# Attention and mixture of experts on one core: norm weights folded, output halves summed on the way out of PSUM, projection over 256 rows

## The chip, the cores and the metric

One core of a Trainium2 chip runs the whole program. The metric is the device time of one execution in microseconds (us). The engines are called PE (matmul and transpose; PEld is its weight load), DVE (VectorE), ACT (ScalarE), POOL (GpSimd) and SP (SyncE, which here only issues DMAs).

## What is computed

The input is x of 8 batches x 256 tokens x 256 features. Two layers follow. The first one is an attention of 16 heads with rotary parts (`L0_attn`) gated by a quantised feed-forward (`L0_ffn`); the change touches it only in a constant and in how the weights of the second layer are prepared. The second layer, cut to what matters:

```python
qkv = einsum('bld,ed->ble', x, w_qkv)         # x here: layer-normalised rows
q = rmsnorm(q, q_norm_w); k = rmsnorm(k, k_norm_w)   # over D = 16, H = 16 heads
scores = einsum('bhqd,bhkd->bhqk', q, k) * D ** -0.5
attn = softmax(scores)
out = einsum('bhqk,bhkd->bhqd', attn, v).transpose(0, 2, 1, 3).reshape(B, L, dim)
attn_out = einsum('bld,ed->ble', out, w_proj) + b_proj
# beside it: 8 routed experts of width 176 (top 2) and a shared one of 352
```

The result of the mixture goes through a gate, is multiplied with attn_out and added to x.

## The kernel before

Every value that enters a matmul is split into a high and a low part of a reduced type (fp32r): ACT copies the high part, DVE or POOL subtracts to get the low one. `product` (lines 55 to 60) makes three matmuls from one: high x high, high x low, low x high. So an operand that comes out of PSUM costs an ACT and a DVE or POOL operation before it can be used.

Three stages run one after the other, each a block with one program per engine. `stage_first` is the feed-forward of layer 0; beside it, ACT and POOL split the weights of the later stages piece by piece (`PIECES`) and SP stores them (`w1_scratch`, `wp_scratch`, ...). POOL also makes nqk = q_norm_w * k_norm_w * scale there, a tile of 128 x 256. `stage_attention0` is the attention of layer 0. `stage_layer1` (line 1079 on) does the second layer.

`stage_layer1` runs over slots n from -16 to 132. Slot n = 16 b + u carries the scores of head u of batch b for n from 0 to 127, and on each engine it does a fixed list in a fixed order. A head's way: scores on PE (L1836, ahead by a slot), negative maximum on DVE (L1696), exponentials on ACT (L1487), reciprocal on DVE (L1728), normalisation on POOL (L1376), transposes on PE (`turn`, L1846), high part on ACT (L1495) and low part on DVE (L1700), product with the values on PE (`values`, L1860). There is one PSUM bank each for scores, turn and output (PO).

Between these each slot has items, taken from `attn_jobs` and from the list of pieces of the mixture. Items of the attention are Q0, Q1, V (projections of the next batch), T (transposes of the normalised rows), X0, X1 (transposes of the scaled q and k), P0, P1 (output projection), L and C (router logits, combine weights). Pieces of the mixture are g, G, u, U (gate and up of a tile, halves of the contraction) and D0, D1 (down). The planner gives each item a cost in units (`COST`) and adds pieces to a slot while the credit of `SLOT_GOAL` units holds, of which 10 (`UNIT`) are the head's own work. The items' PSUM banks are three, in the order of the list (`JOB`, `job_free`).

q and k of a batch: DVE sums the squares (`sum_squares`, L1622), POOL makes three Newton steps (`root_rms`), DVE scales the rows (`scale_rows`, L1635), POOL multiplies q with nqk (`weigh`, L1356), PE transposes (X, L1788, waits for "weighted" and "k_scaled"), ACT and DVE split (L1459, L1575), SP stores to memory (`store_stack`, eight DMAs) and loads the operands of the scores from there, two pairs of heads at a time (`load_stack`, five DMAs). SP's program is one list in which a load that is not due holds back all behind it; `stack_until` puts the stack's transfers between the weight loads, by slot.

The output: four heads share PO. v is spread by POOL over zeroed columns (`vp`) so that head e of a group of four writes 32 rows of PO: 16 for the high part of v and 16 for the low. ACT copies PO to `ot` high (`out_hi`, L1501), DVE subtracts to `ot` low (`out_lo`, L1671). The projection sums high and low rows of four groups, 4 x 128 rows, with the rows of w_proj given twice (`proj_rows`).

## Time and profile before

| what | us |
|---|---|
| median of 3 runs | 1403.62 (1402.06 to 1404.83) |
| the profiled execution | 1404.14 |
| its span | 1402.3 |
| PE busy | 1349.8 (96%) |
| DVE, ACT, POOL busy | 910.4, 752.8, 738.1 |
| second layer: first scores | at 931.97 |

Times in rows are microseconds from the start of the span. "Idle before" is the time an engine did nothing ahead of an instruction, with what ended it. Matmuls overlap, so their durations add up to more than the time between their starts.

### The profile page before, as it was taken

Reading aid. Unit: us, or ns where it says so; the run is one execution under the profiler, and the core shown is the slowest. Engines: PE = TensorE matmul, PEld = TensorE weight load, DVE = VectorE, ACT = ScalarE, POOL = GpSimd, SP = SyncE. Lnnn points to the kernel's source line nnn. Section 1 sums busy time; section 2 is a strip of 40 time slices with the busy share of each in tenths; the row PEclk is TensorE's granted clock in tenths of the full one; section 3 lists DMA queues with packets and bytes.
Section 4 is the critical chain, followed back from the end, with each engine's and each line's share of the span. In section 5 each row is a group of like instructions: output and inputs, shape, how many; then the busy total and the mean of one; then the engine's idle time right before and its main releaser. Section 6 shows DMA issues by size and latency. Waiting matters only on the chain. (4 is left out here: it accounts for less than half of the span.)

```text
span 1402.3 us, 25300 instructions
## 1 busy us (share of the span) xinstructions
PE 1349.8 (96%) x8758; PEld 1201.7 (86%) x8758; DVE 910.4 (65%) x1793; ACT 752.8 (54%) x1948; POOL 738.1 (53%) x725
## 2 busy tenths in 40 slices
PE   9999899999999999999999999879999999999898
PEld 7887798999899989998999898668888888889797
DVE  6655566556656665666565665557887777786765
ACT  4553444545544555445544544246666666666664
POOL 1651333554444545434645453448658676866775
PEclk9999999999999999999999999999999999999999
DMA  5995333324332343233324424166555653645572
GB/s 191 328 329 201 83 91 93 89 77 121 106 89 49 102 138 92 62 90 104 106 65 119 119 65 170 67 173 188 145 177 162 188 173 105 205 149 168 174 196 90
DMA packets 105645, 190.78 MB, mean 136 GB/s; under 512 B 20304, under 2 KB 39440, under 8 KB 103216
## 3 DMA queue, kind: packets, MB, share of 16 engines
q1 hardware_dynamic: 105520, 189.17, 45.0%
q8 instruction: 71, 1.16, 0.4%
q14 instruction: 54, 0.44, 0.1%
HBM read 116.68 MB, written 30.47 MB: 105 GB/s over the span
## 5 line engine op out<-in xcount | busy, mean ns | idle before, releaser
L775 POOL TENSOR_TENSOR a_pr<-a_pr,a_ri 128x512 f32<-128x512 f32 x128 | 133.2, 1041 | 299.5 <-DVE a_ri L955 299.5
L832 ACT ACTIVATE a_pr<-a_score,a_nb 128x256 f32<-128x256 f32 x256 | 119.0, 470 | 267.6 <-DVE a_nb L947 267.6
L1376 POOL TENSOR_TENSOR l_pr<-l_pr,l_ri 128x512 f32<-128x512 f32 x128 | 133.2, 1040 | 121.5 <-DVE l_ri L1728 119.5
L1487 ACT ACTIVATE l_pr<-l_score,l_nb 128x256 f32<-128x256 f32 x256 | 119.1, 471 | 107.7 <-DVE l_nb L1696 107.6
L58 PE MATMUL a_job<-s_xs,s_wh 128*128 128x512 f32 x384 | 153.8, 401 | 1.0 <-PEq L221 1.0
L60 PE MATMUL a_job<-s_xs,s_wl 128*128 128x512 f32 x384 | 151.7, 395 | 0.0
L59 PE MATMUL a_job<-s_xs,s_wh 128*128 128x512 f32 x384 | 151.3, 394 | 0.0
L947 DVE TENSOR_REDUCE a_nb<-a_score 128x2 f32<-128x512 f32 x128 | 88.5, 691 | 85.8 <-PE a_score L1026 84.1
L1696 DVE TENSOR_REDUCE l_nb<-l_score 128x2 f32<-128x512 f32 x128 | 87.5, 684 | 39.4 <-PE l_score L1836 39.2
L960 DVE TENSOR_TENSOR a_pt<-a_turn,a_pt 128x512 fp32r<-128x512 f32 x128 | 87.5, 684 | 23.7 <-ACT a_pt L840 23.7
L1495 ACT ACTIVATE s_wh<-l_turn 128x512 fp32r<-128x512 f32 x128 | 76.9, 600 | 36.3 <-PE l_turn L1846 36.3
L1700 DVE TENSOR_TENSOR s_wh<-l_turn,s_wh 128x512 fp32r<-128x512 f32 x128 | 87.3, 682 | 8.2 <-ACT s_wh L1495 7.7
L1860 PE MATMUL l_out<-s_wh,l_vp 128*128 128x256 f32 x512 | 91.7, 300 | 0.2 <-DVE s_wh L1700 0.2
L58 PE MATMUL l_job<-l_xs,s_wl 128*128 128x512 f32 x224 | 89.6, 400 | 1.9 <-DVE l_vc L1570 1.9
L1846 PE MATMUL l_turn<-s_ident,l_pr 128*128 128x128 f32 x512 | 78.1, 275 | 11.5 <-DVE s_wh L1700 11.1
L60 PE MATMUL l_job<-l_xs,s_wl 128*128 128x512 f32 x224 | 89.0, 397 | 0.0
L59 PE MATMUL l_job<-l_xs,s_wl 128*128 128x512 f32 x224 | 88.6, 396 | 0.0
L955 DVE RECIPROCAL a_ri<-a_sm 128x2 f32<-128x2 f32 x128 | 21.3, 166 | 102.1 <-ACT a_pr L832 102.1
L60 PEld LDWEIGHTS a_job<-s_xs,s_wl 128*128 128x128 f32 x384 | 72.1, 188 | 16.9
L1846 PEld LDWEIGHTS l_turn<-s_ident,l_pr 128*128 128x128 f32 x512 | 58.7, 140 | 29.5 <-issue 14.0
L58 PEld LDWEIGHTS a_job<-s_xs,s_wh 128*128 128x128 f32 x384 | 72.2, 188 | 11.3 <-issue 1.4
L59 PEld LDWEIGHTS a_job<-s_xs,s_wh 128*128 128x128 f32 x384 | 72.4, 189 | 10.3
(251 smaller groups left out, 4569.2 us busy)
## 6 DMA issues: line engine op xcount, KB each, us to landing
s_wl<-wgu_scratch SPq DMA_DIRECT2D x56, 512.0 KB, 5.7
a_sk<-a_rotk SPq DMA_DIRECT2D x384, 64.0 KB, 2.0
a_sq<-a_rotq SPq DMA_DIRECT2D x256, 64.0 KB, 2.0
s_xs<-xn_scratch SPq DMA_DIRECT2D x14, 1024.0 KB, 5.7
l_wd<-wd_scratch SPq DMA_DIRECT2D x56, 256.0 KB, 2.9
l_zq<-qs_scratch SPq DMA_DIRECT2D x128, 64.0 KB, 4.3
l_sk<-ks_scratch SPq DMA_DIRECT2D x32, 256.0 KB, 4.9
a_raw<-in_w SPq DMA_DIRECT2D x30, 256.0 KB, 3.0
```

The lines of the kernel that those rows point to most:

```text
L58: pe.matmul(out, lh, rh, start=first, stop=False)
L59: pe.matmul(out, lh, rl, start=False, stop=False)
L60: return pe.matmul(out, ll, rh, start=False, stop=last)
L775: pool.tensor_tensor(e, e, ri[:, n % 2, :].unsqueeze(2).broadcast_to([P, 2, SEQ]), ALU.mult)\
L832: i = act.activation(pr[:, n % 2, t, :], PS[n % 2][:, t * SEQ:(t + 1) * SEQ], ACT.Exp, bias=nb[:, n % 2, t:t + 1], accum_out=sm[:, n % 2, ...
L947: dve.tensor_reduce(nb[:, (n + 1) % 2, :], PS[(n + 1) % 2][:, :].rearrange("p (t k) -> p t k", t=2), AX.X, ALU.max, negate=True).then_inc( ...
L960: dve.tensor_tensor(pt[:, n % 2, 1, :], PT[:, :], pt[:, n % 2, 0, :], ALU.subtract).then_inc(S["turn_free"], 1)
L1376: pool.tensor_tensor(e, e, ri[:, n % 3, :].unsqueeze(2).broadcast_to([P, 2, SEQ]), ALU.mult)\
L1487: i = act.activation(pr[:, n % 3, t, :], PS[n % NPS][:, t * SEQ:(t + 1) * SEQ], ACT.Exp, bias=nb[:, n % 3, t:t + 1], accum_out=sm[:, n % 3 ...
L1696: dve.tensor_reduce(nb[:, (n + 1) % 3, :], PS[(n + 1) % NPS][:, :].rearrange("p (t k) -> p t k", t=2), AX.X, ALU.max, negate=True).then_in ...
L1846: i = pe.transpose(PT[:, kc * SEQ + t * P:kc * SEQ + (t + 1) * P], pr[:, n % 3, t, kc * P:(kc + 1) * P], ident[:, :])
L1860: i = pe.matmul(PO[:, 0:SEQ], vp[:, kc, a, e * P:(e + 1) * P], pt[:, n % 2, q, kc * SEQ:(kc + 1) * SEQ], start=(e == 0 and kc == 0 and q = ...
```

## The change

It folds nqk into the transposed q: the tile becomes one value for each of 128 rows, and X's copy and subtraction carry it as a scale, so each becomes two operations (q with, k without). `weigh` goes. The first batch has both squares in slot -12, both scalings in slot -9, its X one slot earlier, its first stack loads in slot -5 and not -4, and the two memsets of `zq` on POOL. The columns of `vp` are laid out so that the high parts of a group's four heads fill 64 rows of PO and the low parts the other 64. ACT copies one half, DVE adds the other and writes 64 rows of `os`; two groups make 128 rows, which ACT copies (high) and POOL subtracts (low) once in eight slots. P0 and P1 then contract over two blocks of 128 rows and not four, and come in slots u = 4, 5 and not 3, 4 (but for the last batch). Their cost is 6 units for 12, and the goal of a slot 28.1 for 28.7.

```diff
-VG, VSTRIDE, VBLK = 4, 160, 640
+VG, VB, VSTRIDE, VBLK = 4, 2, 144, 576
+VHALF = VG * D1
-        self.wp = sh.wl[:, 0:2 * VG * D].rearrange("p (q a d) -> p q a d", q=2, a=VG)
+        self.wp = sh.wl[:, 0:2 * VB * D].rearrange("p (q a d) -> p q a d", q=2, a=VB)
-        + [("w", i) for i in range(KC)] + [("p", i) for i in range(2)]
+        + [("w", i) for i in range(KC)] + [("p", 0)]
...
-                        pool.tensor_tensor(sh.nqk[:, :], nw[:, 0:D], nw[:, D:2 * D], ALU.mult).then_inc(S["nqk_raw"], 1)
+                        pool.tensor_tensor(sh.nqk[:, :], nw[:, 0:1], nw[:, 1:2], ALU.mult).then_inc(S["nqk_raw"], 1)
...
-                for i in range(2):
-                    sp.dma_start(l1.wp[:, :, 2 * i:2 * i + 2].bitcast(F32).rearrange("p s a d -> p s (a d)"), wp_dram[i]).then_inc(l1.w_in, 16)
+                sp.dma_start(l1.wp.bitcast(F32).rearrange("p s a d -> p s (a d)"), wp_dram[0]).then_inc(l1.w_in, 16)
...
-    T, Q, V, S_, P_, LOG, CMB, GU, DH = 4, 12, 12, 4, 12, 20, 4, 12, 6
+    T, Q, V, S_, P_, LOG, CMB, GU, DH = 4, 12, 12, 4, 6, 20, 4, 12, 6
-    UNIT, SLOT_GOAL, EARLY_GOAL = 10, 28.7, 18
+    UNIT, SLOT_GOAL, EARLY_GOAL = 10, 28.1, 18
     def X_AT(m):
-        return (9, 10)
+        return (8, 9) if m == 0 else (9, 10)
-        if u in (3, 4) and b >= 1:
-            jobs.append((f"P{u - 3}", b - 1))
+        first = 3 if b == BATCH else 4
+        if u in (first, first + 1) and b >= 1:
+            jobs.append((f"P{u - first}", b - 1))
+        ITEMS[n].sort(key=lambda item: item in (("X0", 0), ("X1", 0)))
+    LOAD_AT = {2 * PER_LOAD * i - (4 if i else 5): i for i in range(N // (2 * PER_LOAD))}
...
-                    if n % (2 * PER_LOAD) == 0 and 0 <= n // (2 * PER_LOAD) + 1 < N // (2 * PER_LOAD):
-                        load_stack(n // (2 * PER_LOAD) + 1)
+                    if n in LOAD_AT:
+                        load_stack(LOAD_AT[n])
...
-                def weigh(m):
-                    pool.wait_ge(S["q_scaled"], m + 1)
-                    pool.tensor_tensor(qk[:, 0], qk[:, 0], sh.nqk[:, :].unsqueeze(1).broadcast_to([P, TB, D]), ALU.mult)\
-                        .then_inc(S["weighted"], 1)
+                def out_lo(k):
+                    pool.wait_ge(S["out_hi"], k + 1)
+                    pool.tensor_tensor(ot[:, 1, k % VB, :], os[:, k % VB, :], ot[:, 0, k % VB, :], ALU.subtract).then_inc(S["out_lo"], 1)
...
                 pool.memset(vp[:, :, :, :].bitcast(F32), 0.0).then_inc(S["vp_zeroed"], 1)
+                pool.wait_ge(S["vp_zeroed"], 1)
+                pool.memset(zq[64:P, 0].bitcast(F32), 0.0).then_inc(S["zeroed"], 1)
+                pool.wait_ge(S["zeroed"], 1)
+                pool.memset(zq[0:64, 1].bitcast(F32), 0.0).then_inc(S["zeroed"], 1)
...
                     if 0 <= n + 1 < N:
                         normalise(n + 1)
+                    if n >= 10 and (n - 10) % 8 == 0 and (n - 10) // 8 < VB * BATCH:
+                        out_lo((n - 10) // 8)
                     for K in HID_AT[n]:
                         hid_lo(K)
...
-                        act.activation(tqk[:, half, :, 0, :], bank[:, :].rearrange("p (r n) -> p r n", r=2), ACT.Copy).then_inc(S["turned_hi"], 1)
+                        act.activation(tqk[:, half, 0, 0, :], bank[:, 0:SEQ], ACT.Copy, scale=sh.nqk[:, 0:1])
+                        act.activation(tqk[:, half, 1, 0, :], bank[:, SEQ:2 * SEQ], ACT.Copy).then_inc(S["turned_hi"], 1)
...
-                def out_hi(g):
+                def out_low(g):
+                    here, there = VHALF * (g % 2), VHALF * (1 - g % 2)
                     act.wait_ge(S["pv_done"], 4 * g + 4)
-                    if g >= VG:
-                        wait_full(act, ("P1", g // VG - 1))
-                    act.activation(ot[:, 0, g % VG, :], PO[:, 0:SEQ], ACT.Copy).then_inc(S["out_hi"], 1)
+                    act.activation(ol[here:here + VHALF, :], PO[there:there + VHALF, 0:SEQ], ACT.Copy).then_inc(S["out_low"], 1)
+
+                def out_hi(k):
+                    act.wait_ge(S["out_free"], 2 * k + 2)
+                    if k >= VB:
+                        wait_full(act, ("P1", k // VB - 1))
+                    act.activation(ot[:, 0, k % VB, :], os[:, k % VB, :], ACT.Copy).then_inc(S["out_hi"], 1)
...
                     if n >= 6 and (n - 6) % 4 == 0 and (n - 6) // 4 < VG * BATCH:
-                        out_hi((n - 6) // 4)
+                        out_low((n - 6) // 4)
                     if 0 <= n + 1 < N:
                         exps(n + 1)
+                    if n >= 10 and (n - 10) % 8 == 0 and (n - 10) // 8 < VB * BATCH:
+                        out_hi((n - 10) // 8)
...
-                def out_lo(g):
-                    dve.wait_ge(S["out_hi"], g + 1)
-                    dve.tensor_tensor(ot[:, 1, g % VG, :], PO[:, 0:SEQ], ot[:, 0, g % VG, :], ALU.subtract).then_inc(S["out_free"], 1)
+                def out_sum(g):
+                    here = VHALF * (g % 2)
+                    dve.wait_ge(S["out_low"], g + 1)
+                    if g >= 4:
+                        dve.wait_ge(S["out_lo"], (g - 4) // 2 + 1)
+                    dve.tensor_tensor(os[here:here + VHALF, g // 2 % VB, :], PO[here:here + VHALF, 0:SEQ], ol[here:here + VHALF, :], ALU.add)\
+                       .then_inc(S["out_free"], 1)
...
-                        if u in ((4, 5) if b < 0 else (2, 3)):
-                            sum_squares(b + 1, u - (4 if b < 0 else 2))
-                        if u == 4 and b < 0:
-                            dve.memset(zq[64:P, 0].bitcast(F32), 0.0).then_inc(S["zeroed"], 1)
-                            dve.memset(zq[0:64, 1].bitcast(F32), 0.0).then_inc(S["zeroed"], 1)
-                        if u in (7, 8):
-                            scale_rows(b + 1, u - 7)
+                        for r in range(2):
+                            if u == (4 if b < 0 else 2 + r):
+                                sum_squares(b + 1, r)
+                        for r in range(2):
+                            if u == (7 if b < 0 else 7 + r):
+                                scale_rows(b + 1, r)
...
-                        pe.wait_ge(S["out_free"], VG * (m + 1))
-                        for a in range(VG):
+                        pe.wait_ge(S["out_lo"], VB * (m + 1))
+                        for a in range(VB):
                             i = product(pe, bank[:, 0:D], [ot[:, q, a, t * P:(t + 1) * P] for q in range(2)],
-                                        [wp[:, q, a, :] for q in range(2)], a == 0, a == VG - 1)
+                                        [wp[:, q, a, :] for q in range(2)], a == 0, a == VB - 1)
```

DVE's subtraction of X is split in the same way as ACT's copy (a `scalar_tensor_tensor` with nqk for q, a `tensor_tensor` for k), and the rows of w_proj in `proj_rows` are given once, eight heads to a block.

## Rows read from the trace of the kernel before

**Rows 1.** The page's head.
```profile
span 1402.3 us, 25300 instructions
```

**Rows 2.** Stretches of the span: PE, PEld, DVE, ACT, POOL busy; clock; DMA share; GB/s.
```profile
932.00:1380.40 448.40, 429.14 (x2927) 383.59 (x2928) 337.42 (x738) 294.56 (x839) 317.45 (x387) 0.99 0.57 169
1380.40:1402.30 21.90, 15.82 (x112) 14.31 (x110) 10.29 (x18) 6.36 (x15) 9.47 (x8) 0.97 0.15 48
```

**Rows 3.** Timeline of the last projection: start, duration, engine, line; 20 starts lie between.
```profile
1394.79 0.28 PE L58 MATMUL l_job<-s_wl,l_ot 128*128 128x256 f32 x1
...
1397.16 0.28 PE L60 MATMUL l_job<-s_wl,l_ot 128*128 128x256 f32 x1
```

**Rows 4.** The chain that ended last, around the first scores: start, time, work.
```profile
901.04 0.91 DVE l_zq L1718
902.67 1.10 DVE l_ss L1622
...
909.59 0.75 DVE l_qk L1635
...
912.46 1.68 DVE l_qk L1635
914.27 0.63 PE l_job L1788 x4
926.38 5.46 DMA l_sk<-ks_scratch
931.97 0.77 PE l_score L1836 x2
```

**Rows 5.** PE ahead of and behind the first scores: timeline, then stretches with granted clock.
```profile
906.50 0.50 PE L58 MATMUL l_job<-l_xs,s_wl 128*128 128x512 f32 x1 [1.92 <-DVE l_vc L1570]
...
936.38 0.52 PE L1836 MATMUL l_score<-l_sk,l_zq 128*128 128x256 f32 x2
...
912.00:914.00 2.00, 0.00 (x0) 1.00 0.11 45
...
930.00:931.00 1.00, 0.00 (x0) 0.50 1.03 336
```

**Rows 6.** SP's issues and POOL's first product with a combine row, in the first batch.
```profile
916.29 0.56 SPq L1271 DMA_DIRECT2D qs_scratch<-l_tqk  x1
...
921.98 0.53 SPq L1256 DMA_DIRECT2D ct_scratch<-l_ct  x1
923.64 0.36 SPq L1265 DMA_DIRECT2D l_cb<-ct_scratch  x1
...
924.52 1.82 SPq L1286 DMA_DIRECT2D l_zq<-qs_scratch  x4
...
927.81 1.26 POOL L1383 TENSOR_TENSOR l_ga<-l_ga,l_cb 128x512 f32<-128x512 f32 x1 [6.70 <-DMA l_cb<-ct_scratch]
```

**Rows 7.** PE's waits in the body (total, times, longest); POOL's product; DVE's scaling, min/median/max.
```profile
PE l_turn L1846 <- DVE s_wh L1700: 11.1, 25, 1.3
...
PE l_job L1788 <- issue: 3.2, 5, 0.7
...
L1356 POOL TENSOR_TENSOR l_qk<-l_qk,s_nqk 128x512 f32<-128x512 f32 x8 | 13.1, 1633 | 0.0
...
L1635 DVE TENSOR_TENSOR l_qk<-l_qk,l_rq x16: 679/812/1827, 909.6 to 1307.9; 128x512 f32<-128x512 f32 x16
```

**Rows 8.** Groups of instructions: count, busy us, mean ns of one, idle before.
```profile
L1387 POOL TENSOR_TENSOR l_hid<-l_ga,l_hid 128x512 fp32r<-128x512 f32 x56 | 72.0, 1285 | 6.3 <-ACT l_hid L1510 6.2
L1501 ACT ACTIVATE l_ot<-l_out 128x256 fp32r<-128x256 f32 x32 | 12.6, 394 | 1.6 <-PE l_out L1860 1.6
L1459 ACT ACTIVATE l_tqk<-l_job 128x512 fp32r<-128x512 f32 x16 | 9.5, 593 | 2.5 <-PE l_job L1788 2.5
```

**Rows 9.** Timeline of the end: POOL's last merge and DVE's last product.
```profile
1396.59 1.29 POOL L1399 TENSOR_TENSOR s_x<-s_x,l_y 128x512 f32<-128x512 f32 x1
...
1398.36 0.69 DVE L1737 TENSOR_TENSOR l_y<-l_y,l_s 128x512 f32<-128x512 f32 x1
```

More of the change, by code:

```diff
@@ L98, in __init__ @@
         self.ident = n.sb("ident", [P, P])
-        self.nqk, self.bp, self.db = (n.sb(s, [P, D]) for s in ("nqk", "bp", "db"))
+        self.bp, self.db = (n.sb(s, [P, D]) for s in ("bp", "db"))
+        self.nqk = n.sb("nqk", [P, 1])
         self.rw = n.sb("rw", [P, 2, KC, E], F32R)
@@ L163, in stage_first @@
     NHID, NRAW, NSPLIT = 3, 4, 3
-    PIECES = [("g", i) for i in range(2)] + [("m", i) for i in range(MT)] + [("w", i) for i in range(KC)] + [("p", i) for i in range(2)]
+    PIECES = [("g", i) for i in range(2)] + [("m", i) for i in range(MT)] + [("w", i) for i in range(KC)] + [("p", 0)]
     PIECES = [("g", 0), ("g", 1)] + [x for i in range(8) for x in (("m", i), ("g", i + 2))] + [("m", i) for i in range(8, MT)] \
-        + [("w", i) for i in range(KC)] + [("p", i) for i in range(2)]
+        + [("w", i) for i in range(KC)] + [("p", 0)]
     PIECE_AT = {}
@@ L1205, in stage_layer1 @@
             "own", "consts", "zeroed", "vp_zeroed", "job_full", "xs_hi", "v_hi", "spread",
-            "sq_ready", "ms_ready", "newton", "q_scaled", "k_scaled", "weighted", "turned_hi",
+            "sq_ready", "ms_ready", "newton", "q_scaled", "k_scaled", "turned_hi",
             "score_full", "max_ready", "exp_ready", "sum_inv", "norm_ready", "turn_full", "turn_hi", "turn_free",
-            "pv_done", "out_hi", "out_free", "tanh_ready", "gate_done", "cmul", "hid_hi", "hid_lo", "down_done",
+            "pv_done", "out_low", "out_free", "out_hi", "out_lo", "tanh_ready", "gate_done", "cmul", "hid_hi", "hid_lo", "down_done",
             "lg_exp", "cm_ready", "y_ready", "y_tanh", "y_act", "gated", "merged", "last_merged", "stored")}
@@ L1574, in job_out @@
                         dve.wait_ge(S["turned_hi"], 2 * m + half + 1)
-                        dve.tensor_tensor(tqk[:, half, :, 1, :], bank[:, :].rearrange("p (r n) -> p r n", r=2),
-                                          tqk[:, half, :, 0, :], ALU.subtract).then_inc(free_of(item), 1)
+                        dve.scalar_tensor_tensor(out=tqk[:, half, 0, 1, :], in0=bank[:, 0:SEQ], scalar=sh.nqk[:, 0:1],
+                                                 in1=tqk[:, half, 0, 0, :], op0=ALU.mult, op1=ALU.subtract)
+                        dve.tensor_tensor(tqk[:, half, 1, 1, :], bank[:, SEQ:2 * SEQ], tqk[:, half, 1, 0, :], ALU.subtract).then_inc(free_of(item), 1)
                     elif name[0] == "P":
@@ L1705, in _ @@
                     if n >= 6 and (n - 6) % 4 == 0 and (n - 6) // 4 < VG * BATCH:
-                        out_lo((n - 6) // 4)
+                        out_sum((n - 6) // 4)
                     if n - 1 in SUM_AT and SUM_AT[n - 1] == NSTEP - 1:
@@ L1782, in do_item @@
                         half = int(name[1])
-                        pe.wait_ge(S["weighted"], m + 1)
+                        pe.wait_ge(S["q_scaled"], m + 1)
                         pe.wait_ge(S["k_scaled"], m + 1)
@@ L1926, in proj_rows @@
     import numpy as np
-    rows = [[(VG * a + p // (2 * D1)) * D1 + p % D1 for p in range(P)] for a in range(VG)]
+    rows = [[(2 * VG * j + p // D1) * D1 + p % D1 for p in range(P)] for j in range(VB)]
     return np.concatenate([w[r] for r in rows], axis=1)
@@ L1986 @@
         "w_qkv": head_columns(i["L1_attn_w_qkv"]).T, "w_proj": proj_rows(i["L1_attn_w_proj"].T),
-        "norm_w": _np.concatenate([_np.tile(_np.repeat(i[f"L1_attn_{s}_norm_w"], 4), 4) for s in "qk"])[None],
+        "norm_w": _np.stack([_np.tile(_np.repeat(i[f"L1_attn_{s}_norm_w"], 4), 2) for s in "qk"], axis=1),
         "b_proj": i["L1_attn_b_proj"][None],
```

14 lines of the change are left out of this document (7 added, 7 removed).

## The prediction

> **What bounds the kernel now.** I read the page's head first, then the stretches of the second layer, then the timelines of the places where PE stands still. The profiled execution took 1404.14 us, of which 1402.3 are the span [rows 1]; the median of the runs is 1403.62, so the sum is made against 1404.14 and 0.5 us come off at the end. In the 448.4 us from the first scores to the last ones PE is busy for 429.14, DVE for 337.42, POOL for 317.45 and ACT for 294.56 [rows 2]. So PE bounds the body: a matmul taken away there is time, nearly one for one, and work added to another engine is free until it holds back something that PE is due to take. Ahead of the body is a stretch that PE does not bound: a chain of DVE, POOL, PE, SP and DMA that ends in the first scores at 931.97, some 5 us after PE's last piece [rows 4, 5]. Behind it are the last 21.9 us, with PE busy for 15.8 [rows 2].
>
> **The projection.** Each of 16 items P0/P1 is 12 matmuls of 256 columns and becomes 6. Between the first row of [rows 3] and the last lie 20 such starts in 2.37 us, 0.118 each, so an item falls from 1.42 to 0.71 us. 14 items lie in the body: 9.9 us. The planner's goal of 28.7 to 28.1 units a slot spreads the freed room: a unit is about one such matmul, and 0.6 x 0.118 x 128 slots is 9.1, the same thing from the other side; the last D1 then comes in slot 128, not 129. It is not one for one, since each slot gets shorter while DVE's work in it does not, and PE is busy for 96%. I take nine tenths, **-8.9**; ends -5 and -10.5.
>
> **The weights folded.** POOL's product of q with nqk goes: 8 times 1633 ns [rows 7]. In the body it stands right ahead of X0, and the five waits of PE put down to "issue" there, 3.2 us together [rows 7], are for it by the code (X waits for "weighted"). Beside it DVE's scaling of rows took up to 1827 ns, where its shortest is 679 [rows 7], and what is queued behind it reaches the next slot's turn late. I count the 3.2 and 1.3 for those, **-4.5**; ends -1 (X0 waits for the scaled k instead) and -8. In its place X's copy on ACT becomes two, 2 x 394 for 593 ns [rows 8], so 16 x 0.2 = 3.1 us on an engine that is busy for 66% of the body; DVE's subtraction becomes two as well, by the same proportion 0.2 more each. X's bank is then free 0.4 us later, with three banks in turn, and its stores that much later, with the loads due three slots on: **+0.5**, ends 0 and +3.
>
> **The output.** ACT's first copy keeps its time (half the partitions, 256 elements, 394 ns [rows 8]), and so does DVE's operation on PSUM. New are 16 copies on ACT from SBUF (394 ns, the nearest row) and 16 subtractions on POOL, at half of 1285 ns [rows 8] 0.65 each, 10.3 us, under the 13.1 that leave. ACT's second copy waits for DVE's sum; behind it on ACT are a gate's tanh and a hidden tile's copy. On POOL the subtraction stands behind the slot's normalisation and ahead of the hidden tile's low half. P waits for out_lo of slot u = 2 and comes in u = 4, so a slot of 448.4/127 = 3.5 us covers a chain of some 2 us. I take **+1**; from below 0, from above 16 x 0.65 = 10. What decides is DVE's 1827 against 679 ns beside a POOL operation [rows 7]: POOL work of 10.3 us replaces 13.1 of the same kind. The Trainium skill, SBUF — State Buffer, section "Who interferes with whom", says that a DVE instruction with two SBUF inputs and a GpSimd instruction that reads SBUF exclude each other for a whole instruction. By that page the subtraction, moved from DVE on PSUM to POOL on SBUF, speaks against this change, and up to 10 us would come back.
>
> **The first batch.** Now: squares of row 0, two memsets of 0.91 us on DVE, squares of row 1 at 902.67, Newton steps on POOL, scaling at 909.59 and 912.46, product, X0 at 914.27 [rows 4]. After the change the second squares follow the first directly and end at 900.6, not 903.8; Newton and the small steps around it take the 5.8 us up to 909.59 and so end at 906.4. V's output, no longer behind the second squares, comes 2 us sooner, and g1, which waited until 906.50 for it [rows 5], with it. DVE is through U0 near 907.1 and scales both rows by 908.9, so X0 is issued near 909, 5.3 us sooner. Routing, G1 and U1 stand ahead of X0's subtractions on DVE: out at 912.9 (before: by 916.29 [rows 6]); X1, whose bank waits for U1, at 914.4. The memsets go to POOL: no row prices them there; between 0.9 us (DVE's) and 2.6 (POOL's 1285 ns for half the columns [rows 8]) each. I take 0.9, done before Newton wants POOL; at 2.6 Newton starts 3 us late.
> On SP four stores of each half take 0.6 us each to issue [rows 6], so the last ends near 917.8. Now the combine's store goes at 921.98, its load at 923.64, the stack's loads at 924.52 [rows 6]; with these due a slot sooner they stand ahead of that store and start near 918.3. sk, issued at 926.38, led to scores 5.6 us later [rows 4]; so the first scores could start near 925.75, 6.2 us sooner. PE's items up to there end near 924.7 (16.5 us of matmuls from 904.4 and some 3.8 of waits), so its idle 5 us shrink to 1. The granted clock was 0.50 (1.2 of 2.4 GHz) at 930 to 931, and the slot from 931.97 to 936.38 took 4.4 us where its matmuls need 2.4 at full rate; in the 3 us without a matmul ahead of X0 the clock stayed at 1.00 [rows 4, 5]. A short idle keeps PE at 2.4 GHz: 2.0 more, 8.2 in all.
> **What is late next** is the first routed expert: D0 of tile 3, in the slot of the first scores, needs POOL's product with the combine row, which started at 927.81, 4.2 us after its load was issued [rows 6]. That load now comes behind five loads, near 922.4: landed at 926.5, product 1.3, ACT 0.6, low half 1.3, so D0 at 929.8, where PE would be there at 927.4. PE loses 2.4 us of the 8.2, and slot 0 starts at 930.5 instead of 936.38 [rows 5]: **-5.9**, ends -3 and -8.5.
>
> **The rest.** At the end, D1 of the last tile now stands ahead of the last turn (+0.7), and the last output goes through ACT, DVE, ACT, POOL (0.4, 0.4, 0.4, 0.65 and hops, 2.0 us), so P0 starts 0.9 us later than now, and the two items are 1.4 us shorter: -0.5. But POOL's last merge, now at 1396.59, comes 0.7 later too, beside DVE's last product at 1398.36 [rows 9]: **0**, ends -0.5 and +1. The first stage splits one piece fewer and reads a far smaller norm_w, on ACT, POOL and SP while PE multiplies: 0, ends -0.5 and +0.5. If PE's wait for it were the last there, the whole gain of a smaller load would be in those 0.5. Sum: -8.9 - 4.5 + 0.5 + 1 - 5.9 = **-17.8**, so 1386.3 on the profiled execution and **1386** against the median.
>
> **The rivals.**
> (A) The body follows DVE, not PE. For it: the turn's 25 waits for DVE's low half, 11.1 us, are the body's largest idle [rows 7]. Against: 96%. Then the projection gives -5 and the product -2: 1404.1 - 5 - 2 + 1.5 - 5.9 = 1392.7, 1392 by the median.
> (B) More than forecast: the X slots lose all their waits (-8) and the combine's load lands in time (-8.2): 1404.1 - 9.9 - 8 - 8.2 + 1 = 1379.
> (C) Slower, by ACT's queue: out_hi waits there for DVE's sum with hid_hi, tanh and the next turn's copy behind it, and POOL's subtraction delays hid_lo, so that D waits. It makes the kernel slower when one of 16 such places costs over (17.8 + 1)/16 = 1.2 us; at twice its own work (2 x (0.39 + 0.65) = 2.1 us) the time is 1404.1 - 18.8 + 33 = 1418. Against it: ACT is idle for a third of the body, and a D follows its U by a slot or more.
> (D) It does not do what it says: the loads of the first stack land no sooner and the freed units turn into idle; -2 to -4, so 1401.
>
> **How the numbers follow.** Forecast (1381 to 1391) 0.54; A (to 1396) 0.20; B 0.17; D 0.05, half of it within 0.2% (2.8 us, about what a measurement of this kernel can tell from no change); C 0.04. The range 1378 to 1394 takes in B's 1379, A's 1392 and the first batch's bounds. Faster 0.94, same 0.03, slower 0.03.
>
> **What would show it.** First scores near 926, the clock at 1.00 through 940; PE waiting about 2 us for POOL's low half at the first routed D; no idle "issue" ahead of X0; 96 matmuls fewer on the three product lines; 435 us from first to last scores for 448.4. It is wrong if the first scores come after 929, if PE's idle in the body grows by over 5 us, or if turns wait on DVE in the slots of out_hi.

## The result, and the profile after

Four runs of the changed kernel gave a median of **1411.09 us** (1407.11 to 1412.16), beside 1403.11 for the kernel before in runs on the same chip: ratio **1.0045** [1.0032, 1.0058]. The change makes the kernel 0.45% slower, 8 us, where 17.8 us less were forecast. The profiled execution took 1407.11, the fastest of the four, so the trace shows some 3 of the 8 us. The mean granted clock of the four was 0.994, 0.991, 0.990 and 0.989, from the fastest to the slowest; the kernel before had 0.997 in its profiled execution, and 0.995 by the median of its executions in the batches below.

The page's head, to stand beside [rows 1] and the table of before:

```profile
span 1405.0 us, 25173 instructions
PE 1345.8 (96%) x8662; PEld 1194.3 (85%) x8662; DVE 911.1 (65%) x1807; ACT 765.2 (54%) x1979; POOL 736.7 (52%) x734
```

The work went as the diff says: PE's busy time fell by 4 us and its share is 96% as before. The stretches of the second layer in the changed kernel (busy time of PE, PEld, DVE, ACT, POOL, clock, DMA share, GB/s), from layer 1's first transposes to the first scores, on to slot 0, the body, the end, to stand beside [rows 2]:

```profile
889.13:921.97 32.84, 30.49 (x167) 24.48 (x167) 21.14 (x56) 12.51 (x24) 15.31 (x23) 1.00 0.38 129
921.97:931.17 9.20, 4.46 (x14) 3.69 (x15) 1.34 (x3) 2.58 (x7) 4.63 (x6) 0.65 0.88 268
931.17:1381.57 450.40, 420.91 (x2833) 373.22 (x2833) 339.37 (x751) 304.20 (x863) 315.17 (x392) 0.99 0.55 166
1381.57:1405.00 23.43, 14.17 (x97) 12.28 (x95) 11.45 (x18) 6.76 (x16) 10.12 (x9) 0.95 0.13 44
```

First scores came at 921.97, not 931.97; slot 0 at 931.17, not 936.38 [rows 5]. Then the body of 126 slots took 450.40 us, where before it took 444.0 (936.38 to 1380.39), with less PE work in it. The sum of PE's waits in this body, to stand beside [rows 7]:

```profile
PE l_turn L1867 <- DVE s_wh L1722: 18.6, 30, 2.1
PE l_down L1777 <- DVE l_y L1700: 4.9, 2, 3.6
PE l_job L1822 <- DVE l_xs L1583: 3.3, 3, 1.3
```

The waits for "issue" ahead of X are gone, as forecast. The turn's waits for DVE grew from 11.1 to 18.6, and two waits that were worth nothing before now cost 8.2 together.

**Where in the body.** From PE's timeline I took the start of the first score matmul of each slot, and so each slot's length. Slots with the same u have the same work for the attention; summed over slots 0 to 125 (us):

| kernel | u 3-5 | 6-8 | 9-10 | 11-12 | 13-15 | 0-2 | body |
|---|---|---|---|---|---|---|---|
| before | 83.9 | 83.0 | 63.2 | 57.3 | 74.9 | 81.7 | 444.0 |
| the change | 89.2 | 87.1 | 55.4 | 58.8 | 80.1 | 79.9 | 450.4 |

So the halved projection (u 3 to 5) made its own slots longer; the folded weights show their gain at u 9-10; and u 6-8 and 13-15, where the diff changes little but the planner's choices, grew by 9. The largest single place is slot 29, 8.56 us for 3.25. PE's timeline there:

```profile
1037.46 0.55 PE L1777 MATMUL l_down<-l_wd,l_hid 128*128 128x256 f32 x1 [3.57 <-DVE l_y L1700]
1037.81 0.41 PE L1778 MATMUL l_down<-l_wd,l_hid 128*128 128x256 f32 x1
...
1042.28 0.28 PE L1777 MATMUL l_down<-l_wd,l_hid 128*128 128x256 f32 x1
```

D0 of a group's first tile may start only when DVE has taken the last group's sum out of its bank (L1700). The new cost and goal moved D0 to the head of slot 29; before, it came later. PE stood 3.57 us, and the next matmuls took 0.41 for 0.28 us; the granted clock in these stretches of the changed kernel:

```profile
1036.00:1037.00 1.00, 0.00 (x0) 0.00 (x0) 1.00 (x3) 0.84 (x4) 0.00 (x0) 1.00 0.00 0
...
1038.00:1039.00 1.00, 1.00 (x7) 1.00 (x6) 0.00 (x0) 0.58 (x1) 0.94 (x1) 0.50 0.06 16
```

**The clock in the body, which this one trace shows at its mildest.** Behind its first 0.4 us, this body had a granted clock of 0.50 twice: at 1037.4 to 1040.8, and at 1081.7 to 1085.1, behind a turn's wait of 2.09 us for DVE. PE was busy for 6.7 us of it. In the kernel before the clock was at half only in the body's first 0.24 us. The variant with the loads in slot -4 (below) has the same items in its body, and its profiled execution took 1412.02. There such stretches add up to 17 us:

```profile
1036.85:1043.68 6.83, 5.90 (x22) 5.25 (x23) 2.20 (x5) 2.47 (x7) 1.04 (x1) 0.50 0.01 2
1125.60:1129.01 3.41, 3.41 (x18) 3.41 (x18) 1.49 (x6) 0.72 (x2) 3.10 (x7) 0.50 0.02 4
1241.65:1248.48 6.83, 6.83 (x34) 6.83 (x34) 3.71 (x15) 2.64 (x11) 4.76 (x11) 0.50 0.00 0
```

Slot 84, first in the change's trace, then in that variant's. The longest wait in it is the same, 1.28 and 1.27 us for T's low part (`l_xs`, L1583):

```profile
1235.87:1241.01 5.14, 3.86 (x35) 3.69 (x34) 4.65 (x13) 2.77 (x8) 3.46 (x5) 1.00 0.36 84
1238.28:1244.93 6.65, 5.38 (x34) 5.20 (x33) 4.71 (x13) 3.10 (x9) 4.74 (x8) 0.75 0.33 91
```

It took 5.14 us at a clock of 1.00, and 6.65 at 0.75; slot 85 behind it took 3.28 and 4.87. So the same work with the same waits was 3.1 us dearer in one execution than in the other, and one trace does not give the price of the change. Matmuls of 256 columns start 0.21 us apart at half clock, for 0.12 at full; so, as an estimate, the 16.1 us in which PE was busy in the three stretches cost some 7, where the 6.7 of the change's own trace cost some 3.

**Where the first batch's gain stopped.** SP's issues and PE's first item behind the first scores, in the changed kernel:

```profile
915.21 0.60 SPq L1277 DMA_DIRECT2D ks_scratch<-l_tqk  x1
...
916.48 1.84 SPq L1291 DMA_DIRECT2D l_zq<-qs_scratch  x4
918.37 0.56 SPq L1293 DMA_DIRECT2D l_sk<-ks_scratch  x1
...
921.34 0.35 SPq L1270 DMA_DIRECT2D l_cb<-ct_scratch  x1
921.74 0.42 SPq L1250 DMA_DIRECT2D s_wl<-wgu_scratch  x1
...
927.19 0.77 PE L59 MATMUL l_job<-l_xs,s_wl 128*128 128x512 f32 x1 [4.75 <-DMA s_wl<-wgu_scratch]
```

The stores ended at 915.8, 2 us before my estimate, and the scores came 3.8 us before it. But the gate and up weights of tile 5 are issued behind the stack's loads, the combine row's store and its load, at 921.74, and PE stood 4.75 us for them.

### The profile page after: what moved, and what is told of

Read it like the earlier page. It is cut to its first block and busy times, and to the rows that moved or that the text cites. A ratio compares the mean times of both kernels' runs of the same rounds, so it can differ in the third digit from the quotient of the medians.

```text
span 1405.0 us, 25173 instructions
## 1 busy us (share of the span) xinstructions
PE 1345.8 (96%) x8662; PEld 1194.3 (85%) x8662; DVE 911.1 (65%) x1807; ACT 765.2 (54%) x1979; POOL 736.7 (52%) x734
## 5 line engine op out<-in xcount | busy, mean ns | idle before, releaser
L1867 PE MATMUL l_turn<-s_ident,l_pr 128*128 128x128 f32 x512 | 78.1, 275 | 19.4 <-DVE s_wh L1722 18.6
L60 PEld LDWEIGHTS a_job<-s_xs,s_wh 128*128 128x128 f32 x384 | 72.2, 188 | 10.5
```

What stands on the lines that cost most here:

```text
L60: pe.matmul(out, lh, rl, start=False, stop=False)
L1867: i = pe.transpose(PT[:, kc * SEQ + t * P:kc * SEQ + (t + 1) * P], pr[:, n % 3, t, kc * P:(kc + 1) * P], ident[:, :])
```

## The experiments

Unless it is said otherwise, medians stand beside the kernel before in the same batch, ratios with their 95% interval. Bodies and slots are from the profiled execution of each.

### The planner's two numbers

**The change without them** (P costs 12 again, goal 28.7):

```diff
-    T, Q, V, S_, P_, ... = 4, 12, 12, 4, 6, ...
-    UNIT, SLOT_GOAL, EARLY_GOAL = 10, 28.1, 18
+    T, Q, V, S_, P_, ... = 4, 12, 12, 4, 12, ...
+    UNIT, SLOT_GOAL, EARLY_GOAL = 10, 28.7, 18
```

> The change with only the planner's two numbers put back (P cost 12 and SLOT_GOAL 28.7 units); P keeps its slots 4 and 5 and its 6 matmuls. Theory PLAN (the new numbers line pieces of the mixture up behind ACT, DVE and POOL work, above all D0 of tile 14 first in slot 29, where it waited 3.57 us for the sum of y): the body loses most of its extra stalls, first to last scores 450.4 us falls to 432 to 440, time 1393 to 1400. Theory OUTPUT (the longer chain ACT, DVE, ACT, POOL and the extra operations make the stalls): stalls stay, time 1407 or more.

1410.0, ratio 1.0039 [1.0024, 1.0054]. The old numbers alone give back about 1 us (the change had 1.0045). Slot 29 is back at 3.28 us, and the body is still 453.9: now u 11-12 take 63.2 for 58.8. Of the body's 3.5 us above the change's, some 3 are the clock: PE was busy at 0.50 for 13.0 us, for 7.1 there.

**The kernel before with only the two new numbers** (the reverse edit):

> The kernel before with only the planner's two numbers of the change (P cost 6, SLOT_GOAL 28.1), its P items still 12 matmuls in slots 3 and 4. Theory PLAN: slower than before, by 8 to 20 us (1411 to 1423), with stalls of PE on DVE's low half of the turn grown by 5 us or more. Theory OUTPUT: within 3 us of before, 1400 to 1406.

1413.04 for 1404.66, ratio 1.0058 [1.0043, 1.0073]: two constants, nothing else, cost 8 us. Slot 29 took 8.62 us here too.

**The change with D0 of a group's first tile last in its slot**, where the planner puts it first (slots 29 and 66):

```diff
+    for s in range(1, NSTEP):
+        for n in SLOTS:
+            if ("D0", MT * s) in ITEMS[n] and ITEMS[n][0] == ("D0", MT * s):
+                ITEMS[n] = ITEMS[n][1:] + ITEMS[n][:1]
```

> The change with D0 of the first tile of a step put last in its slot where it stood first (slots 29 and 66), so that DVE's sum of y is done when PE asks. Theory PLAN for slot 29 (excess 5.4 us, PE idle 3.57 and then at half clock): 4 to 6 us faster than the change, 1404 to 1407. If the sum of y holds back what follows anyhow: the same as the change.

1406.62 for 1404.39, ratio 1.002 [1.0009, 1.0031]: against the change's 1.0045 some 3.5 us better. The wait is shorter, not gone:

```profile
1038.65 0.36 PE L1781 MATMUL l_down<-l_wd,l_hid 128*128 128x256 f32 x1 [2.19 <-DVE l_y L1704]
```

Slot 29 took 6.22 us for 8.56. The body is as long as the change's all the same, 450.7: slots 21, 53 and 85 took 4.80, 4.38 and 4.80 us for 3.27 in the change's trace, with the granted clock at 0.50 for a part of each.

### The projection alone

Half of P's matmuls taken out of the kernel before, every copy and subtraction left in place (the sum runs over two of the four groups, so half of the projection is left out):

```diff
-                        for a in range(VG):
+                        for a in range(2):
```

> The kernel before with each P item multiplying two of its four blocks (the output leaves out half of the attention's projection), nothing else changed: 6 matmuls for 12 in slots 3 and 4, the output's chain as before. If PE bounds those slots: 9 to 10 us less, 1394. If DVE bounds them (90% busy in the slots 35 and 36 of the kernel before): the time falls by 0 to 3 us, 1401 to 1404, and the slots u = 3 and 4 keep their lengths, with PE idle.

1402.18 for 1404.61, ratio 0.9982 [0.9971, 0.9994]: **2.4 us**, where 8.9 were forecast of 9.9. The two slots 35 and 36 hold P0 and P1 of a batch. First the stretch in the kernel before, and, for comparison, one without T or P:

```profile
1059.26:1066.10 6.84, 6.62 (x54) 6.01 (x52) 6.15 (x16) 4.24 (x13) 4.82 (x5) 1.00 0.84 230
...
1141.00:1160.80 19.80, 19.80 (x137) 18.19 (x136) 14.32 (x32) 14.60 (x42) 12.35 (x14) 1.00 0.68 214
```

and the same two slots with half of P:

```profile
1059.42:1066.30 6.88, 5.44 (x42) 4.66 (x41) 6.18 (x16) 4.26 (x13) 4.82 (x5) 1.00 0.82 226
```

Twelve matmuls fewer, PE busy for 1.2 us less, and the slots not a moment shorter: DVE is busy for 6.15 us of 6.84, 90%, where in the stretch without T or P it is busy for 72%. Its timeline in slots 51 and 52 of the kernel before shows with what:

```profile
1117.19 0.69 DVE L1696 TENSOR_REDUCE l_nb<-l_score 128x2 f32<-128x512 f32 x1
1117.80 0.68 DVE L1700 TENSOR_TENSOR s_wh<-l_turn,s_wh 128x512 fp32r<-128x512 f32 x1
1118.39 1.13 DVE L1622 TENSOR_REDUCE l_ss<-l_sqr 128x32 f32<-128x512 f32 x1
...
1119.87 0.68 DVE L1566 TENSOR_TENSOR l_xs<-l_job,l_xs 128x512 fp32r<-128x512 f32 x1
...
1120.54 0.40 DVE L1583 SCALAR_TENSOR_TENSOR l_s<-l_job,s_bp 128x256 f32<-128x256 f32 x1
```

The squares of a row of q and k (1.1 us, one row in each of the slots u = 2 and 3), T's low part and the projection's own output come in these slots. They are DVE's. The projection's matmuls filled PE's time beneath them and were nearly free: PE's turns wait longer for DVE instead, 16.8 us in this body for 11.1.

**With the planner's new numbers** on top (half of the projection left out again):

> As e13 with the planner's two numbers of the change (P cost 6, goal 28.1), so that the freed room is filled with the mixture's pieces. If filling gives the room back: 8 us or more less than e13. If the new plan costs what it did in e2 (+8 with 12 matmuls): about the same as e13 or slower, 1402 to 1410.

1407.08, ratio 1.0017 [1.0004, 1.0029]: 4.9 us above the kernel with half of P alone. So the numbers cost 5 even where the matmuls that they count are gone.

### The weights folded, and the first batch

**The fold alone, on the kernel before** (nqk as one value for each row, `weigh` gone, X split in two on ACT and DVE):

```diff
-                        act.activation(tqk[:, half, :, 0, :], bank..., ACT.Copy)
+                        act.activation(tqk[:, half, 0, 0, :], bank[:, 0:SEQ], ACT.Copy, scale=sh.nqk[:, 0:1])
+                        act.activation(tqk[:, half, 1, 0, :], bank[:, SEQ:2 * SEQ], ACT.Copy)
...
-                            weigh(b + 1)
```

> The kernel before with the norm weights folded and nothing else (same plan). My term: -4.5 + 0.5, so 1399, ends 1395 and 1405; the five waits issue ahead of X0 (3.2 us) gone. If the split of X on ACT and DVE is what costs: 1403 to 1407.

**1398.95** for 1404.66, ratio 0.9959 [0.9943, 0.9975]: -5.7, forecast -4.0. PE's waits in this body (935.6 to 1376.4), where the "issue" line is gone and the turn's wait is as before:

```profile
PE l_turn L1842 <- DVE s_wh L1696: 10.9, 28, 1.2
PE l_down L1752 <- DVE l_y L1674: 1.4, 2, 0.7
PE l_score L1832 <- DMA l_sk<-ks_scratch: 0.6, 1, 0.6
PE l_job L1784 <- DVE l_qk L1631: 0.6, 1, 0.6
```

Slots u 9-10 fell from 63.2 to 57.9, and u 11-12 grew by 1.8. I put these down to the split of X, counted at 0.5; no run has the fold without the split.

**The change with the first batch as before** (both squares, scaling, X and the loads back in their slots; the two memsets stay on POOL):

> The change with its first batch put back (squares, scaling, X and stack loads in the slots of before; the memsets stay on POOL). Theory FIRST GAINS (slot 0 started at 931.2 in the change and at 936.4 before): 4 to 6 us slower than the change, 1414 to 1416. Rival (the clock's fall and the wait of 4.75 us for the gate weights of tile 5 behind the stack's loads take the gain back): the same as the change within 2 us.

1411.8, ratio 1.0046 [1.0029, 1.0063]: level with the change's 1.0045. Slot 0 starts at 931.87, only 0.7 us later than in the change, although its first scores come at 928.11 and not at 921.97: here the slot of the first scores takes 3.77 us, in the change 9.20.

**The change with the first stack's loads in slot -4 again**:

> The change with the first stack's loads due in slot -4 again and not -5 (all else as the change). Its slot of the first scores took 9.2 us, 4.75 of it waiting for the gate weights of tile 5, whose load stood behind five stack loads. If that order is the cause: weights and combine rows land sooner, first scores 1 to 3 us later, slot 0 starts at 929 to 931 and the time is the same or 1 to 2 us less. Rival (DMA queues are full whatever the order): the wait moves to the stack's own landing, slot 0 at 932 to 934, the time 1 to 2 us more.

1409.92 for 1403.55, ratio 1.0039 [1.0026, 1.0051]; first scores at 927.41 for 921.97, slot 0 at 931.48 for 931.17. Loads a slot sooner bring the first scores 5.4 us sooner and slot 0 only 0.3.

**Fold and first batch together, on the kernel before**:

> The kernel before with the fold and the change's first batch, without the output's half. The change's slot 0 started 3.6 us sooner after its stage's begin than before, e3's 1.3 us sooner. Theory FIRST GAINS: 1 to 3 us less than e3 (1396 to 1398 where e3 had 1399). Rival (given back in the slot of the first scores, as e4 suggested): e3 within 1 us.

1398.64 for 1404.61, ratio 0.9956 [0.994, 0.9973], beside 0.9959 for the fold alone. The first scores come at 925.02 for 931.29 with the fold alone, slot 0 at 934.61 for 935.69, 1.1 us sooner; the last scores come 0.4 sooner (1375.87, 1376.31), and the medians differ by 0.3.

### The output's two parts

**The output half alone, on the kernel before**: groups of two blocks, ACT, DVE, ACT, POOL, P0 and P1 of six matmuls in u = 3, 4, the planner's old numbers.

```diff
+                    act.activation(ol[here:here + VHALF, :], PO[there:there + VHALF, 0:SEQ], ACT.Copy)
+                    dve.tensor_tensor(os[here:here + VHALF, g // 2 % VB, :], PO[...], ol[...], ALU.add)
+                    act.activation(ot[:, 0, k % VB, :], os[:, k % VB, :], ACT.Copy)
+                    pool.tensor_tensor(ot[:, 1, k % VB, :], os[...], ot[:, 0, k % VB, :], ALU.subtract)
```

> The kernel before with only the output's half of the change (vp's layout, sum leaving PSUM, P over 256 rows), every item in the slot of before (P in 3 and 4, cost 12, goal 28.7) and the weights' product kept on POOL; zq's memsets on POOL. 14 items in the body are 0.71 us shorter. Theory OUTPUT (the longer chain stalls the slots u = 10 to 12, where ACT copies os ahead of X1 and DVE's reciprocal waits behind X1's subtraction): the slots 10 to 12 of each batch lose 1 us or more beyond before, time 1400 to 1406. Theory PLAN alone: 1393 to 1396.

1413.74 for 1403.55, ratio 1.0069 [1.0054, 1.0084].

**The same with the fold**:

> As the kernel before in plan and first batch, with both the fold and the output's half of the change (so all the change's arithmetic and none of its placement). If the parts add up (fold gave -5.7 alone): e5 less 5.7. Theory PLAN: 1388 to 1391. Theory OUTPUT with X's split (both load ACT in slot 10): 1398 to 1404, and less than the sum of the parts' gains.

1409.0, ratio 1.0039 [1.0027, 1.005]. The fold gives its 5 us again; against the fold alone the output half **costs 11** (ratios 1.0039 and 0.9959), although it takes away the matmuls that were worth 2.4. PE and POOL in slot 35 of this kernel:

```profile
1059.94 0.36 PE L59 MATMUL l_job<-s_wl,l_ot 128*128 128x256 f32 x1 [2.38 <-POOL l_ot L1380]
```

```profile
1058.07 1.04 POOL L1375 TENSOR_TENSOR l_pr<-l_pr,l_ri 128x512 f32<-128x512 f32 x1 [3.45 <-DVE l_ri L1748]
1059.07 0.73 POOL L1380 TENSOR_TENSOR l_ot<-l_os,l_ot 128x256 fp32r<-128x256 f32 x1
```

P0 in u = 3 needs a subtraction that stands on POOL behind this slot's normalisation, and that waits 3.45 us for DVE's reciprocal behind the squares. u 3-5 take 90.8 for 83.9.

**P0, P1 in u = 4, 5**, as the change has them, the rest as above:

```diff
+    for m in range(BATCH - 1):
+        at = H1 * (m + 1) + 3
+        k = ITEMS[at + 1].index(("P1", m))
+        ITEMS[at].remove(("P0", m))
+        ITEMS[at + 1][k] = ("P0", m)
...
+        ITEMS[at + 2].insert(k, ("P1", m))
```

> As e6 (fold and output's half, plan and first batch of before), with P0 and P1 one slot later (4, 5) and every other item left in its slot. In e6 slots u = 3 lose 18.2 us against 2.4 before, PE waiting there for POOL's low half of os. If that wait is the cost: the 16 us come back, time 1391 to 1395. If the chain costs wherever P stands: 1400 or more.

1409.5 for 1404.39, ratio 1.0034 [1.0023, 1.0046]: as dear. P0 does not wait now, but look at the slots one by one (sums over all eight batches):

| kernel | u = 3 | u = 4 | u = 5 |
|---|---|---|---|
| fold alone: 12 + 12 matmuls in u = 3, 4 | 27.1 | 31.1 | 25.5 |
| this one: 6 + 6 in u = 4, 5 | 28.2 | 32.3 | 30.8 |

Slot 3 has lost all 12 matmuls and got no shorter, since DVE sets it. Slot 5 has got 6 and is 5.3 us longer over seven batches, where 7 x 0.71 is 5.0: 0.46 to 0.71 in six of them, and 1.6 in slot 85, where the clock was at 0.50. Slot 4 has 6 in place of 12 and is 1.2 us longer in all, since slot 84 took 7.58 us for 4.76, with a part of it at half clock too. "One slot later" moves the projection out from under DVE's work into a slot that PE bounds. This trace is of the longest of the nine executions, 1412.99 us for a median of 1409.5, so bodies held against its 452.4 flatter the others.

**The output's high copy and subtraction of u = 10 two slots later**, in u = 12, first with P in u = 3, 4, then in u = 4, 5:

```diff
+    OUT_AT = {8 * k + (10 if k % 2 else 12): k for k in range(VB * BATCH)}
```

> As e6, with the one copy and subtraction of os that fell in slot u = 10 two slots later (u = 12), away from X1; the other stays at u = 2. Theory OUTPUT by collision with X1: 4 to 8 us faster than e6, and the slots 10 to 12 back to what e3 (fold alone) shows. If the operations cost wherever they stand: the same as e6 within 2 us.

> As e9, with the copy and subtraction of os that fell in u = 10 two slots later. e7 against e6 gained 1.2 us in the median and 4 us in the slots 11 and 12. Expected: e9 less 1 to 4 us, 1388 to 1393, faster than the kernel before and than the fold alone (1399). If the collision with X1 is nothing: the same as e9.

1407.76, 1.0027 [1.0016, 1.0038], and 1408.16, 1.002 [1.0011, 1.003]: each 1.3 us below its own pair by the medians, some 2 by the ratios, 3.2 and 4.3 in the profiled bodies, the second of them against that 452.4. What it takes away is seen in the change's slot 27, where ACT's new copy stands ahead of X's two (L1516, L1468, L1469). ACT, DVE, POOL and PE there:

```profile
1024.31 0.42 ACT L1516 ACTIVATE l_ot<-l_os 128x256 fp32r<-128x256 f32 x1
1024.63 0.46 ACT L1468 ACTIVATE l_tqk<-l_job,s_nqk 128x256 fp32r<-128x256 f32 x1
1024.99 0.38 ACT L1469 ACTIVATE l_tqk<-l_job 128x256 fp32r<-128x256 f32 x1
```

```profile
1025.40 0.48 DVE L1592 SCALAR_TENSOR_TENSOR l_tqk<-l_job,s_nqk,l_tqk 128x256 fp32r<-128x256 f32 x1 [1.12 <-ACT l_tqk L1469]
1025.80 0.42 DVE L1594 TENSOR_TENSOR l_tqk<-l_job,l_tqk 128x256 fp32r<-128x256 f32 x1
1026.13 0.15 DVE L1749 RECIPROCAL l_ri<-l_sm 128x2 f32<-128x2 f32 x1
```

```profile
1026.36 1.04 POOL L1376 TENSOR_TENSOR l_pr<-l_pr,l_ri 128x512 f32<-128x512 f32 x1 [2.61 <-DVE l_ri L1749]
1027.37 1.17 POOL L1381 TENSOR_TENSOR l_ot<-l_os,l_ot 128x256 fp32r<-128x256 f32 x1
```

```profile
1029.30 0.63 PE L1867 MATMUL l_turn<-s_ident,l_pr 128*128 128x128 f32 x4 [1.78 <-DVE s_wh L1722]
```

ACT's copy holds X's copies, DVE waits 1.12 us for them with the reciprocal queued behind, POOL waits 2.61 for the reciprocal, and PE's next turn loses 1.78. The split of X alone makes a part of this chain: in the fold alone DVE waits 0.76 at this place, and the next turn loses 0.62.

**The change with both repairs** (D0 last, late copy):

> As e11, with the copy and subtraction of os of u = 10 at u = 12 as in e10. Slots 11 of the change lose 5.8 us against 2.5 before. Expected: e11 less 1 to 4 us; if slot 11's loss is X's split alone (the fold without the output had 4.3 there): e11 within 1 us.

1406.78 for 1404.39, ratio 1.0013 [1.0002, 1.0024]. Still not as fast as before. Its ten executions had a granted clock of 0.990 by the median, for 0.995.

**The change with P at u = 6, 7**, and both repairs:

> The change with P in slots 6 and 7 (all but the last batch), the swap of e11 and the late copy of e12. Theory COVER (P placed where DVE is 70% busy and PE is the bound, freed slots 3 to 5 filled by pieces): 4 us or more faster than e12, under 1403. Rival (L's transposes then wait uncovered for T's low half in slot 4, as they do in the change for 1.3 us): the same as e12 or slower, slot u = 4 at 7 us excess or more.

1410.88 for 1404.61, ratio 1.0039 [1.0026, 1.0052]. The logits' item L in u = 4 is left without a matmul ahead of it while DVE works: its waits for T's low part are 5.4 us in the body, 3.3 with P in u = 4, 5. The body grows by more, from 447.4 to 454.1, and most of that is the clock: it was at 0.50 for 23.9 us of this body, for 10.2 of the other, and PE was busy in 22.8 and 10.2 of them, which makes some 6 us of time (an estimate, by the same two distances). In the change the wait of L is there already, in slot 52:

```profile
1122.61 0.36 PE L1822 MATMUL l_job<-s_rw,l_xs 128*128 128x16 f32 x2 [1.28 <-DVE l_xs L1583]
```

L needs T's low part. In the kernel before P1's 12 matmuls stood ahead of L in this slot, and it took 4.33 us without a wait of PE; in the change P0's 6 stand there, and it takes 5.14.

**POOL's subtraction last in its slot**, then **a subtraction of 8 columns for 256** (the second leaves out the low part of the attention's output), both on the kernel with P in u = 4, 5:

```diff
-                    pool.tensor_tensor(ot[:, 1, k % VB, :], os[:, k % VB, :], ot[:, 0, k % VB, :], ALU.subtract)
+                    pool.tensor_tensor(ot[:, 1, k % VB, 0:8], os[:, k % VB, 0:8], ot[:, 0, k % VB, 0:8], ALU.subtract)
```

> As e9 with POOL's subtraction of os behind the slot's other POOL work (low half of the hidden tile, product with the combine row) and not ahead of it. Theory POOL ORDER: 3 us or more faster than e9, the slots u = 3 to 5 back towards 87 us. Rival (ACT's copy ahead of X1, T and the hidden tile's copy): the same as e9 within 2 us.

> As e9, with the subtraction over 8 columns and not 256 (P multiplies the high part in its place, so the low part of the attention's output is left out); all waits stay. Theory POOL: POOL is freed for 16 x 0.6 us and DVE beside it, 5 us or more faster than e9. Rival (ACT): the same as e9 within 2 us, and what e9 loses against the fold alone is ACT's second copy and DVE's order.

1406.77 and 1406.58 for 1403.84, ratios 1.0029 [1.0014, 1.0045] and 1.0014 [1.0002, 1.0026], where the full subtraction in its old place had 1.0034. By the ratios that is 0.7 us for the order, with an interval that takes in no gain, and 2.8 for nearly the whole subtraction. (Bodies: 448.7 and 449.5 for 452.4, but that one comes from 1412.99 us again, and 2.6 and 2.2 us of the difference are slot 84 alone.) So POOL's share is some 3 us, and it is not shown that a change of order recovers it. What is left is not POOL's. The waits in the body with the subtraction last:

```profile
PE l_turn L1873 <- DVE s_wh L1728: 23.9, 34, 1.9
...
PE l_job L59 <- POOL l_ot L1387: 1.1, 2, 0.5
```

The turn's waits on DVE are 13 us above the fold alone (10.9): summed by slot, those of u = 3 grew from 0.4 to 10.5, up to 1.9 each, where P0's 12 matmuls used to be, and those of u = 11 from 2.4 to 4.6. The 10 us at u = 3 are not lost time: these slots grew by 1.1 us in all, since DVE sets their length with or without the matmuls.

## Why the prediction was wrong

**The body's bound.** The step that failed is the first: "So PE bounds the body: a matmul taken away there is time, nearly one for one". It was read from one row of 448 us [rows 2]. 96% is a mean over slots of two kinds, and P sits in the kind where DVE is the bound. One more stretch of two slots, with DVE at 90%, would have told it. Projection: forecast -8.9, ends -5 and -10.5; measured -2.4, outside both.

**The clock.** The prediction counts the clock once, as a gain of the first batch, and puts it at nothing in the body. Nearly every stretch at half clock in the bodies of the change and its variants stands a few us behind waits of PE that the change uncovered: D0's, L's and the turns' for DVE. The change's executions had a mean granted clock of 0.9905 by the median, the kernel before 0.995. That is 13 and 7 us of full-speed time not granted ((1 - clock) x the time of an execution). The difference of 6 us is an estimate from above, since what is not granted while PE waits costs nothing, and it stands beside a loss of 8. That the waits bring the fall down is argued from their order in the traces. No run removed them all, and with the same waits slot 84 kept a clock of 1.00 in one execution and lost it in another.

**The planner.** I took its 0.6 units a slot for a second proof of the gain ("the same thing from the other side"), and gave its choices no term. The two numbers alone cost 8.4 us on the kernel before and 4.9 with half of P gone. Of the first, 5.0 are slots 27 to 29 (16.4 us for 11.3), where D0 waits 3.6 us for a sum that cost at most 0.7 before; the rest was not divided further. In the changed kernel the same reversal gave only 1: slot 29 is mended there, and other slots grow (u 11-12 by 4.4). Moving the one item gave 3.5.

**The output.** Forecast +1, with an upper end of 10; measured +11 against the fold alone, by ratios, though 2.4 us of saved matmuls are in that. The price was set by cover, not by the chain's own time. I asked whether a slot of 3.5 us covers the chain, and it does; I did not ask what P's move uncovers. Slot 5 pays 5 us, slot 3 gives nothing back. With P left in u = 3 and 4 its waits for POOL cost as much. A further 1 (medians) to 3 (bodies) are ACT's copy ahead of X, and some 3 POOL's. These overlap, and their sum is not a measured split. What the Trainium skill, SBUF — State Buffer, "Who interferes with whom", states of DVE instructions with two SBUF inputs and GpSimd instructions that read SBUF is borne out in kind: one 128x256 subtraction took 1.17 us beside such a DVE instruction. The size that I took from it, up to 10 us, is not: the other 15 took 0.73 to 0.78, most of them beside DVE work with at most one input in SBUF, and removing nearly all of the subtraction gave about 3.

**The weights folded.** Right: forecast -4.5 and +0.5, measured -5.7. The waits for "issue" went, as the code said. The split of X is +1.8 in its slots, near four times my +0.5, within its ends.

**The first batch.** The mechanism was right up to the first scores: 6.4 us sooner from the layer's start than with the first batch as before, for a forecast of 6.2. Slot 0 at 931.17 for a forecast 930.5 looks like a hit and is luck: with the first batch as before it came at 931.87. The slot of the first scores took 9.20 us for 3.77 and gave the 6.4 back but for 0.9; beside the fold alone 6.7 sooner and 5.2 longer leave 1.5. (In six kernels that share this part the way from the layer's start to slot 0 was 43.1 to 44.6 us, so these remainders are no more than the spread.) Two things were wrong. The transfer that is late next is not the combine's row but tile 5's weights, issued one place behind it on SP; and "a short idle keeps PE at 2.4 GHz" did not come about: PE's idle of 4.75 us only moved from ahead of the first scores to behind them, and with it the lower clock. Of the 5.2 us at slot 0, 1.6 come from the earlier start of the layer and 0.9 from the first batch; the rest is in the fold (1.3 in its own trace) and in what was not tried alone, such as the memsets on POOL. The medians agree: with the first batch as before the change runs level, and beside the fold it brings 0.3. Forecast -5.9, measured between 0 and -1. The clock's rows in the changed kernel:

```profile
926.00:927.00 1.00, 0.00 (x0) 0.00 (x0) 0.00 (x0) 0.00 (x0) 0.99 (x1) 0.50 1.04 344
930.00:931.00 1.00, 1.00 (x7) 1.00 (x6) 0.24 (x1) 0.87 (x2) 1.00 (x4) 0.50 1.07 256
932.00:933.00 1.00, 1.00 (x6) 0.77 (x6) 0.97 (x3) 0.49 (x3) 1.00 (x2) 1.00 1.03 275
```

**The rest.** The first stage and layer 0, forecast 0, became some 1.6 us shorter (layer 1 starts at 889.13 for 890.75; in the fourteen kernels with one piece of w_proj at 888.8 to 891.7, in the six others at 889.7 to 891.8, so one trace of each does not tell whether it goes with the piece that is not split, and this was not tried alone). The end, forecast 0, became 1.5 longer, just above its upper end of +1: P0 started there at 1397.98, 16.4 us behind the last scores, after four hops, where it started at 1394.79, 14.4 behind them [rows 3]. POOL's merge stood at 1399.61 for 1396.59 [rows 9]:

```profile
1397.05 0.78 POOL L1381 TENSOR_TENSOR l_ot<-l_os,l_ot 128x256 fp32r<-128x256 f32 x1 [5.71 <-ACT l_ot L1516]
...
1399.61 1.26 POOL L1403 TENSOR_TENSOR s_x<-s_x,l_y 128x512 f32<-128x512 f32 x1
```

**The rivals.** Rival A (the body follows DVE) was right in kind, and still priced the projection at -5 from the mean. Rival C (ACT's queue ahead of other work) exists at u = 11, at 1 to 3 us and not 33. It had the direction right, at 0.04. No rival had a projection that loses its cover, and none had the planner or the clock in the body. What gave it away in my own list of signs: turns waiting on DVE, and PE's idle in the body, which grew by 10 us (from 19.3 to 29.5) where 5 was the limit.

**The sum.** By ratios: the fold -5.7, the output half with its projection on top +11.2 (1.0039 against 0.9959), and from there to the change, with P later, the planner's numbers and the first batch, +0.8 (1.0045). That makes 6.3 us, the ratio's 0.45%; the two medians differ by 8.

**The version to keep** is the fold alone, or with the first batch: 1398.95 and 1398.64, ratios 0.9959 and 0.9956, faster than both kernels.

## What to carry to other kernels

Before a matmul is priced as time, read the two or three slots in which it stands, not the stage: if another engine is busy for 90% there, the matmul is cover. Taking it away gains little, and moved to a slot that PE bounds it costs its full length there. A wait that loses its cover can cost more than its own length, when the granted clock falls behind it: read the clock in the body, and in more than one execution. A planner's cost and goal are a change of their own: run them alone on the old kernel first, and look for the items whose waits they uncover.

## What the runs showed of the hardware

- PE's clock after an idle of 3.57 us at 1033.9 to 1037.5 was at 0.50 until 1040.8 (matmul 0.41 for 0.28 us), while in the kernel before the idle ahead of X0, with no matmul from 912 to 914, left it at 1.00 [rows 5]. The slot grew by 5.3 us for a wait of 3.57.
- The clock fell behind short waits too, and not in every execution. In the change with D0 last it was at 0.50 from 1005.6 to 1009.0, where PE's waits in the 7 us before were 0.39, 0.70 and 0.30 us; with the same waits in that place the change's own trace has 1.00. Four executions of the change, of one program, had 0.989 to 0.994.
- A POOL subtraction of 128x256 from SBUF took 0.73 to 0.78 us in 15 of 16 places and 1.17 where it lay beside DVE's L1615, which took 0.88 there for a median of 0.69.
